# A delta-rule layer on one core: the chain over chunks in blocks of 4 steps with the decay added in PSUM, and the stage ahead of it spread over separate buffers

## The chip, the core and the metric

The kernel runs on one core of a Trainium2 chip. The metric is the device time of one execution, in microseconds (us), from launch to the last write. The core has a matmul engine (TensorE, PE in the profile; its weight loads are listed as PEld), a vector engine (DVE), a scalar engine (ACT), GpSimd (POOL) and a queue engine (SyncE, SP), which here issues nearly all of the DMA transfers. Each engine runs its own list of instructions and waits on semaphores.

## What is computed

Two transformer-like layers over 4096 tokens (two sequences of 2048) of width 256, all in float32 at the interfaces. The first is attention and a mixture of experts, the second a gated delta rule with 16 heads of width 16, a small MLP and a soft mixture of experts. The change touches the delta rule alone:

```python
def step(Sst, inp):
    q_t, k_t, v_t, b_t, g_t = inp
    Sst = Sst * g_t[..., None, None]                      # decay
    kS = jnp.einsum('bhk,bhkv->bhv', k_t, Sst)
    Sst = Sst + b_t[..., None, None] * jnp.einsum('bhk,bhv->bhkv', k_t, v_t - kS)
    o_t = jnp.einsum('bhk,bhkv->bhv', q_t, Sst)
    return (Sst, o_t)
_, out = jax.lax.scan(step, S0, (qt, kt, vt, bt, gt))     # over 2048 tokens of a sequence
```

## The kernel before

The program is a row of phases, each a function that hands every engine its own list of work; between phases all engines meet. The scan over tokens is done in chunks of 16 tokens (`CL`): within a chunk by products that need no earlier state, from chunk to chunk by a chain. Three phases prepare it (`phase_gram`, `phase_lanes`, `phase_mix`), and `phase_chain` runs the chain over the 128 chunks of a sequence, both sequences at once.

**phase_mix** goes over 32 tiles of 128 tokens. For a tile t, SP loads three tensors (`pr` L1942, `tp_in` L1943, `fac_in` L1945); ACT widens `tp_in` into `wide` (L2040); POOL scales k, v and q (L1973 to L1986); PE multiplies 64 blocks of 32x32 (`first`, L2004), ACT keeps the product in `nat` (L2047); PE multiplies 64 blocks again (`second`, L2016), DVE keeps that (L2070, L2072); PE turns two of the four results (L2024) and the decays (L2026) in the same stage as `second`, and ACT keeps them as `w_q` (L2054) and `gam_col` (L2056), the tables that the chain reads. SP stores `u_o` (L1951) and `k_end` (L1955). Inputs have two buffers, so the load of tile t waits until tile t-2 is scaled and widened; one set of PSUM tiles per parity (`ps`) is used by `first`, `second` and the turns in turn, so `first` of a tile waits until ACT has kept `w_q` of the tile before the last.

**phase_chain** keeps the state in SBUF in four sets (2 sequences x 2 halves of the heads). A step, for one chunk, is: PE multiplies the state by the chunk's `w` (L2182, 8 blocks of 32x32 for each sequence b), DVE subtracts that from `u_in` (L2226, one for each b), PE multiplies the result by `k_in` (L2192, 8 blocks for each b) into `ps_u`, and DVE makes the new state of b with two operations (L2233), one for each half of the 32 rows, as `ps_u` times a 0/1 mask plus `faded`. `faded` is the old state times the chunk's decay, made by ACT (L2209, four a step) beside it. Steps come in blocks of `CB` = 16; for each block SP issues 12 loads (L2131 two and L2133 one for each set) and 4 stores (L2142), and POOL copies the block's part of `w_q` and `gam_col` (L2162, L2163). All have two buffers: the load of block t waits until block t-2 is done.

`staged(eng, n, *stages, unroll=2)` (L87) writes an engine's list: stage s of round r works on tile r-s; `unroll` rounds stand in the body of a hardware loop (`Fori`, L101), and the rounds that don't fill the loop are written out before and behind it. So the body of PE's loop holds two tiles in phase_mix and two blocks, 32 steps, in phase_chain. A float32 32x32 product is two matmuls with a weight load each in the trace.

Rounds of SP in both phases: the load of round r, then the store of an earlier one, in that order.

Of the kernel before, what the change touches and what calls it, by code (L numbers as in the profile page):

```python
# [11 lines left out]
ALU = mybir.AluOpType  # L12
# [3 lines left out]
P = 128  # L16
D = 256
# [34 lines left out]
class Transfers:  # L52
# [24 lines left out]
    def before(self, t, p):  # L77

        return t * (16 * self.per) + (32 - 16 * p) * self.per
# [58 lines left out]
class Phase:  # L138
# [24 lines left out]
    def transfers(self, name, per=1, soft=False):  # L163
        return Transfers([self.sem(f"{name}{p}", soft) for p in range(2)], per, soft)
# [1724 lines left out]
def phase_mix(nc, sems, proj, t_p, factors, halves, w_q, gam_col, u_o, k_end, ident):  # L1889

    HG = H // 4
    with Phase(nc, "mix", sems) as ph:
        pr = ph.sb("pr", [P, 2, PW])
        tp_in = ph.sb("tp_in", [P, 2, 2 * H, CL])  # L1900
        fac_in = ph.sb("fac_in", [P, 2, 2, H])
# [5 lines left out]
        gam_k = ph.sb("gam_k", [P, 2, H, HD])  # L1907
# [4 lines left out]
        landed = ph.transfers("landed", 3)  # L1912
        widened = ph.steps("widened", 2)
        scaled = ph.steps("scaled", 6)
# [5 lines left out]
        w_q_kept = ph.steps("w_q_kept", KD + 1)  # L1920
# [12 lines left out]
        def _(sp):  # L1933
            for s in (landed, stored):
                s.prime(sp)

            def load(t, p):
                sp.wait_ge(scaled.sem, scaled.before(t))
                hold(sp, gate)
                sp.wait_ge(widened.sem, widened.before(t))  # L1940
# [7 lines left out]
            def store(t, p):  # L1948
                sp.wait_ge(y_kept.sem, y_kept.at(t))
                hold(sp, gate)  # L1950
                sp.dma_start(u_o[bass.ds(t * P, P)].rearrange("n a x -> n (a x)"),  # L1951
                             nat[:, p, 1:3].rearrange("q a h d -> q (a h d)")).then_inc(stored.sems[p], 32)
                sp.wait_ge(scaled.sem, scaled.at(t))
                hold(sp, gate)
                sp.dma_start(k_end[bass.ds(t * P, P), :], k_out[:, p].rearrange("q h d -> q (h d)")).then_inc(stored.sems[p], 32)  # L1955
            staged(sp, NT, load, idle, store)
# [4 lines left out]
        def _(pool):  # L1961
            scaled.prime(pool)

            def scale(t, p):
                q, k, v_in = [pr[:, p, i * D:(i + 1) * D].rearrange("q (h d) -> q h d", h=H) for i in range(3)]
                beta = pr[:, p, 3 * D:3 * D + H]

                def wide_of(x):
                    return x.unsqueeze(2).to_broadcast([P, H, HD])
# [3 lines left out]
                pool.tensor_tensor(b_gam[:, p, :], beta, fac_in[:, p, 0, :], ALU.mult).then_inc(scaled.sem, 1)  # L1973
                pool.tensor_tensor(k_v[:, p, :, 1, :], v_in, wide_of(beta), ALU.mult).then_inc(scaled.sem, 1)
                pool.wait_ge(scaled.sem, scaled.at(t, 1))
                hold(pool, gate)
                pool.tensor_tensor(k_v[:, p, :, 0, :], k, wide_of(b_gam[:, p, :]), ALU.mult).then_inc(scaled.sem, 1)  # L1977
                pool.wait_ge(y_kept.sem, y_kept.before(t))
                hold(pool, gate)
                pool.tensor_tensor(q_gam[:, p, :, :], q, wide_of(fac_in[:, p, 0, :]), ALU.mult).then_inc(scaled.sem, 1)  # L1980
                pool.wait_ge(turned.sem, turned.before(t))
                hold(pool, gate)
                pool.tensor_copy(gam_k[:, p, :, :], wide_of(fac_in[:, p, 0, :])).then_inc(scaled.sem, 1)
                pool.wait_ge(stored.sems[p], stored.before(t, p))
                hold(pool, gate)
                pool.tensor_tensor(k_out[:, p, :, :], k, wide_of(fac_in[:, p, 1, :]), ALU.mult).then_inc(scaled.sem, 1)  # L1986
            staged(pool, NT, scale)

        @block.tensor
        def _(pe):  # L1990
            for s in (firsts, seconds, turned):
                s.prime(pe)

            def first(t, p):
                pe.wait_ge(widened.sem, widened.at(t))
                pe.wait_ge(scaled.sem, scaled.at(t, 3))
# [1260 lines left out]
```

## Time and profile before

| | |
|---|---|
| median of 3 runs | 5107.75 us (5103.05 to 5109.47) |
| the profiled execution | 5108.61 us, of which its span is 5106.9 us |
| mean granted TensorE clock | 0.837 of full speed |
| busy over the span | PE 73%, PEld 39%, DVE 54%, ACT 41%, POOL 1172.7 us |
| instructions | 109157 |
| phase_mix, from PE's first product to the first memset of the chain | 3403.4 to 3638.2 us |
| phase_chain, from that memset to its last state | 3638.2 to about 4093.5 us |

Shares of busy time are means over a dozen phases, of which attention alone is 1.5 ms, so they say nothing on the two phases at hand; these are read by stretch. Idle time is given with what ended it; "issue" there means that an engine had nothing to wait for that the profile shows, and still did not go on. In lists in order of time, equal instructions are merged, and the second figure is how long the merged ones took from the first's start to the last's end.

### The profile page before, as it was taken

The page shows a single profiled execution, that of the slowest core. Times are in us where ns is not written, and L with a number is a line of the kernel's source. Part 1 is how long each engine was busy: PE and PEld are TensorE (multiplying, and loading weights), DVE is VectorE, ACT ScalarE, POOL GpSimd, SP SyncE. Part 2 cuts the span into 40 slices and gives each one's busy share as a digit, 9 for nine tenths or more (in the row PEclk, how much of TensorE's full clock was granted, in tenths as well). Part 3 has the DMA queues.
Part 4 walks back from the last instruction along what each step waited for, and adds up shares of the span by engine and source line. Part 5 has one row for each costly group of instructions (what it writes and reads, how often), then busy time and mean ns, then how long its engine had stood idle before and what let it go on. Part 6 is the DMA issues. An engine that isn't in the chain of part 4 may idle for free. (4 is left out here: it accounts for less than half of the span.)

```text
span 5106.9 us, 109157 instructions
## 1 busy us (share of the span) xinstructions
PE 3737.7 (73%) x37201; PEld 1984.0 (39%) x37203; DVE 2733.6 (54%) x5646; ACT 2108.3 (41%) x3466; POOL 1172.7 (23%) x2077
## 2 busy tenths in 40 slices
PE   6699999999999995528585447026444469789999
PEld 3233333333333332416363226016333346444478
DVE  5688888888888884812123654751133434423433
ACT  0177777777777774214242213013222212243322
POOL 4321121121122110162003730724200013311100
PEclk8799999999999997769797765557555579889999
DMA  1400000000000002044533323334433110040053
GB/s 44 168 35 0 0 0 0 0 0 0 0 0 0 0 0 78 25 156 152 173 119 103 116 84 122 90 106 161 86 42 46 23 56 4 11 157 25 4 186 131
DMA packets 256377, 319.78 MB, mean 63 GB/s; under 512 B 27729, under 2 KB 177489, under 8 KB 256209
## 3 DMA queue, kind: packets, MB, share of 16 engines
q1 hardware_dynamic: 243920, 283.86, 19.0%
q0 software_dynamic: 12288, 33.57, 2.0%
q8 instruction: 119, 1.95, 0.2%
q14 instruction: 50, 0.40, 0.0%
HBM read 181.58 MB, written 135.79 MB: 62 GB/s over the span
## 5 line engine op out<-in xcount | busy, mean ns | idle before, releaser
L791 DVE TENSOR_REDUCE att_maxes<-att_ps_m 128x1 f32<-128x512 f32 x2048 | 1342.0, 689 | 337.2 <-PE att_ps_m L648 324.0
L755 ACT ACTIVATE att_prob<-att_ps_s 128x1024 f32<-128x1024 f32 x1024 | 992.7, 1021 | 439.5 <-PE att_ps_s L658 429.5
L648 PE MATMUL att_ps_m<-att_k_t,att_q_t 96*128 96x512 bf16 x2048 | 792.8, 387 | 22.4 <-DVE att_maxes L791 4.8
L658 PE MATMUL att_ps_s<-att_q_t,att_k_t 99*128 99x512 bf16 x2048 | 612.6, 380 | 1.8 <-ACT att_q_t L741 1.7
L670 PE MATMUL att_ps_o<-att_prob,att_v_h 128*32 128x512 f32 x4096 | 546.3, 605 | 0.8 <-DVE att_o_sum L804 0.5
L648 PEld LDWEIGHTS att_ps_m<-att_k_t,att_q_t 96*128 96x128 bf16 x2048 | 196.6, 96 | 696.9 <-DVE att_maxes L791 595.0
L562 POOL CAST att_max_parts<-att_neg_max 128x4 bf16<-128x4 f32 x128 | 24.7, 193 | 1306.6 <-DVE att_neg_max L798 1306.6
L1359 DVE TENSOR_TENSOR experts_h<-experts_gs,experts_ps_g 128x128 f32<-128x128 f32 x192 | 55.4, 288 | 468.3 <-ACT experts_gs L1340 466.4
L658 PEld LDWEIGHTS att_ps_s<-att_q_t,att_k_t 99*128 99x128 bf16 x2048 | 190.7, 98 | 206.4 <-issue 31.7
L2209 ACT ACTIVATE chain_faded<-chain_state,chain_gam 128x32 f32<-128x32 f32 x512 | 126.6, 311 | 330.0 <-DVE chain_state L2233 320.6
L1312 PE MATMUL experts_ps_g<-w_gu,experts_x_t 128*128 x768 | 217.9, 406 | 35.6 <-ACT experts_x_t L1336 18.9
L2004 PE MATMUL mix_ps<-mix_k_v,mix_wide 32*32 32x32 f32 x4096 | 62.1, 236 | 241.7 <-POOL mix_k_v L1977 209.0
L2182 PE MATMUL chain_ps_w<-chain_state,chain_w 32*32 32x32 f32 x4096 | 96.6, 244 | 154.9 <-issue 85.6
L1575 PE MATMUL comb_ps_p<-comb_w_s,comb_h_t 128*128 128x512 f32 (+1 forms) x256 | 108.3, 583 | 129.4 <-DVE comb_pr L1530 123.0
L1305 PE MATMUL experts_ps_t<-ident,experts_xs 128*128 128x128 f32 x384 | 74.8, 278 | 165.6 <-DMA experts_xs<-slots_x 165.6
L2192 PE MATMUL chain_ps_u<-chain_u,chain_k_in 32*32 32x32 f32 x4096 | 95.0, 244 | 115.7 <-issue 89.6
L2233 DVE SCALAR_TENSOR_TENSOR chain_state<-chain_ps_u,halves,chain_faded 128x32 f32<-128x32 f32 x512 | 98.3, 245 | 130.2 <-PE chain_ps_u L2192 124.1
L1312 PEld LDWEIGHTS experts_ps_g<-w_gu,experts_x_t 128*128 128x128 f32 x768 | 131.3, 191 | 86.9 <-issue 76.1
L2226 DVE TENSOR_TENSOR chain_u<-chain_u_in,chain_ps_w 64x128 f32<-64x128 f32 x256 | 73.0, 285 | 160.2 <-PE chain_ps_w L2182 155.3
L2004 PEld LDWEIGHTS mix_ps<-mix_k_v,mix_wide 32*32 32x32 f32 x4096 | 58.6, 151 | 244.0 <-issue 244.0
L1466 POOL DMA_INDIRECT comb_y_in<-slots_y,pos x128 | 144.7, 1130 | 37.8 <-issue 36.6
L1336 ACT COPY experts_x_t<-experts_ps_t 128x256 f32<-128x256 f32 x192 | 72.4, 377 | 182.3 <-PE experts_ps_t L1305 181.8
(346 smaller groups left out, 6398.5 us busy)
## 6 DMA issues: line engine op xcount, KB each, us to landing
slots_x<-zeros SPq DMA_DIRECT2D x97, 256.0 KB, 3.3
experts_xs<-slots_x SPq DMA_DIRECT2D x48, 512.0 KB
slots_y<-experts_y SPq DMA_DIRECT2D x48, 512.0 KB
logits_t<-sstat_logit SPq DMA_DIRECT2D x64, 256.0 KB
xf_t<-logits_t SPq DMA_DIRECT2D x8, 2048.0 KB
proj<-comb_pr SPq DMA_DIRECT2D x8, 1600.0 KB
mix_pr<-proj SPq DMA_DIRECT2D x32, 400.0 KB
w_d<-in_L_ffn_wd SPq DMA_DIRECT2D x2, 4096.0 KB, 20.0
```

Source lines behind the costliest of these rows:

```text
L648: pe.matmul(ps_m[i % 2][:, :], q_t[0:PAIRS, p, tile * P:(tile + 1) * P], k_t[0:PAIRS, p, c * W:(c + 1) * W], start=True, stop=True).then_i ...
L658: mm = pe.matmul(ps_s[half][:, i * W:(i + 1) * W], k_t[0:ROWS, p, tile * P:(tile + 1) * P], q_t[0:ROWS, p, chunk * W:(chunk + 1) * W], sta ...
L670: mm = pe.matmul(ps_o[i * VW:(i + 1) * VW, :], v_h[:, p, group * GK + i, :], prob[:, (j * NH + i // 2) % RING, i % 2, :], start=(group == ...
L755: nc.scalar.activation(prob[:, i % RING, :, :].rearrange("q a w -> q (a w)"), ps_s[half][:, :], ACT.Exp, scale=SCALE).then_inc(expd.sem, 1)
L791: v.tensor_reduce(maxes[:, p, tile, c:c + 1], ps_m[i % 2][:, :], X, ALU.max).then_inc(reduced.sem, 1)
L1312: mm = pe.matmul(ps_g[p % 2][:, 0:2 * HID], x_t[:, p % 2, k, :], w_gu[:, k, bass.ds(e, 1), :, :].rearrange("q a i h -> q (a i h)"), start= ...
L1466: pool.indirect_dma_start(out=y_in[:, p, i, y, :], out_offset=None, in_=slots_y, in_offset=bass.IndirectOffsetOnAxis(ap=pos[:, t * GT + i, ...
L1575: mm = pe.matmul(ps_p[i % 2][:, a:b], h_t[:, k, i * P:(i + 1) * P], w_s[:, k, a:b], start=(k == 0), stop=(k == KD - 1))
L2004: mm = pe.matmul(ps[p][own, group, 32 * i:32 * i + 32], wide[own, p, place(h), :, :].rearrange("q a t -> q (a t)"), k_v[own, p, h, :, :].r ...
L2182: mm = pe.matmul(ps_w[32 * s:32 * s + 32, j, 0:32], w[own, p, s, c, :], state[own, c % 2, s, :, :].rearrange("q e d -> q (e d)"), start=Tr ...
L2209: nc.scalar.activation(faded[:, s, :, :], state[:, c % 2, s, :, :], ACT.Copy, scale=gam[:, p, s, c:c + 1]).then_inc(fades[b].sem, 1)
L2233: v.scalar_tensor_tensor(state[:, 1 - c % 2, sets, e, :], ps_u[:, sets, HD * e:HD * (e + 1)], halves[:, e:e + 1], faded[:, sets, e, :], AL ...
```

## The change

In phase_mix the three inputs get four buffers instead of two (`LOADS`), and the hardware loop holds four tiles instead of two on SP, POOL, PE and ACT. `first`, `second` and the turns write to PSUM tiles of their own (`ps_x`, `ps_y`, `ps_t`), and `turn` is a stage of its own, one tile behind `second`. The widening is split: four ACT operations of half the size, two ahead of `first` and two ahead of `second`. POOL's scaling is two stages. The decays are no longer turned tile by tile (`gam_k`, L1983, L2026 and L2056 go): one strided load fetches the decays of all chunks' ends at the phase's start, POOL widens them, PE turns them with four products, ACT keeps them at the end of the phase.

In phase_chain `CB` is 4 instead of 16, so SP's 16 transfers come every 4 steps, each a quarter of the size, and PE's loop body holds 8 steps. POOL makes, for each set, `fade`: a 32x32 diagonal matrix for each chunk and block of heads. In place of ACT's `faded`, PE multiplies the state by these diagonals (16 more blocks a step, between the two products of before) into `ps_u`, and the `k_in` product is added on top of it in PSUM. DVE's two operations for the new state of b become one, `ps_u` times a 0/1 mask. ACT has no work left in the phase.

```diff
-    HG = H // 4
+    LOADS = 4
...
+        ends = ph.sb("ends", [P, B, H])
+        ends_wide = ph.sb("ends_wide", [P, B, H, HD])
...
-        ps = [ph.ps(f"ps{i}", [P, HG, GP]) for i in range(2)]
+        ps_x = [ph.ps(f"ps_x{i}", [P, GP]) for i in range(2)]
+        ps_y = [ph.ps(f"ps_y{i}", [P, GP]) for i in range(2)]
+        ps_t = [ph.ps(f"ps_t{i}", [P, GP]) for i in range(2)]
+        ps_e = ph.ps("ps_e", [P, GP])
...
-            staged(sp, NT, load, idle, store)
+            staged(sp, NT, load, idle, idle, store, unroll=LOADS)
...
-            staged(pool, NT, scale)
+            staged(pool, NT, scale_kv, scale_qk, unroll=LOADS)
...
             def first(t, p):
-                pe.wait_ge(widened.sem, widened.at(t))
-                pe.wait_ge(scaled.sem, scaled.at(t, 3))
-                pe.wait_ge(w_q_kept.sem, w_q_kept.before(t))
+                pe.wait_ge(wide_t.sem, wide_t.at(t))
+                pe.wait_ge(kv_scaled.sem, kv_scaled.at(t))
+                pe.wait_ge(x_kept.sem, x_kept.before(t))
...
             def second(t, p):
                 pe.wait_ge(x_kept.sem, x_kept.at(t))
+                pe.wait_ge(wide_p.sem, wide_p.at(t))
+                pe.wait_ge(y_kept.sem, y_kept.before(t))
...
+            def turn(t, p):
                 pe.wait_ge(y_kept.sem, y_kept.at(t))
-                pe.wait_ge(scaled.sem, scaled.at(t, 5))
+                pe.wait_ge(w_q_kept.sem, w_q_kept.before(t))
...
-            staged(pe, NT, first, second)
+            staged(pe, NT, first, second, turn)
...
-            staged(act, NT, widen, keep_x, keep_w_q)
+            staged(act, NT, widen_t, idle, keep_x, idle, keep_w_q, unroll=LOADS)
...
-CB = 16
+CB = 4
...
-                    pool.tensor_copy(gam[:, p, s, :], gam_col[:, half, own]).then_inc(fetched.sem, 1)
+                    pool.tensor_tensor(fade[:, p, s, :, :], eye[:, :].unsqueeze(1).to_broadcast([P, CB, 32]),
+                                       gam_col[:, half, own].unsqueeze(2).to_broadcast([P, CB, 32]), ALU.mult).then_inc(fetched.sem, 1)
...
+                    for s in range(SETS):
+                        for j in range(4):
+                            own = slice(32 * j, 32 * j + 32)
+                            mm = pe.matmul(ps_u[own, s, 0:32], fade[own, p, s, c, :], state[own, c % 2, s, :, :].rearrange("q e d -> q (e d)"),
+                                           start=True, stop=False, skip_group_check=True)
+                    mm.then_inc(faded.sem, 1)
                     for b in range(B):
                         pe.wait_ge(us[b].sem, us[b].at(t, c + 1))
+                        pe.wait_ge(faded.sem, faded.at(t, c + 1))
...
                                 mm = pe.matmul(ps_u[32 * j:32 * j + 32, s, 0:32], k_in[own, p, c, cols], u[own, p, c, cols],
-                                               start=True, stop=True, skip_group_check=True)
+                                               start=False, stop=True, skip_group_check=True)
...
-            def chunks(t, p):
-                act.wait_ge(fetched.sem, fetched.at(t))
-                for c in range(CB):
-                    for b in range(B):
-                        act.wait_ge(states[b].sem, states[b].at(t, 2 * c))
-                        for s in range(KD * b, KD * b + KD):
-                            nc.scalar.activation(faded[:, s, :, :], state[:, c % 2, s, :, :], ACT.Copy,
-                                                 scale=gam[:, p, s, c:c + 1]).then_inc(fades[b].sem, 1)
...
-                        v.wait_ge(fades[b].sem, fades[b].at(t, KD * (c + 1)))
-                        for e in range(2):
-                            v.scalar_tensor_tensor(state[:, 1 - c % 2, sets, e, :], ps_u[:, sets, HD * e:HD * (e + 1)], halves[:, e:e + 1],
-                                                   faded[:, sets, e, :], ALU.mult, ALU.add).then_inc(states[b].sem, 1)
+                        v.tensor_tensor(state[:, 1 - c % 2, sets, :, :].rearrange("q s e d -> q s (e d)"), ps_u[:, sets, 0:32],
+                                        own_half[:, :, :].rearrange("q e d -> q (e d)").unsqueeze(1).to_broadcast([P, KD, 32]),
+                                        ALU.mult).then_inc(states[b].sem, 1)
```

## Rows read from the trace of the kernel before

**Rows 1.** Busy time by stretch: us, PE, PEld, DVE, ACT, POOL, clock, DMA share, GB/s

```profile
3403.00:3433.00 30.00, 17.21 (x912) 16.24 (x912) 2.27 (x6) 8.19 (x20) 12.08 (x25) 0.52 0.32 102
3433.00:3610.00 177.00, 116.71 (x6864) 112.35 (x6864) 19.00 (x51) 65.81 (x181) 75.47 (x153) 0.75 0.48 159
...
3657.00:3767.00 110.00, 46.92 (x2048) 34.15 (x2048) 42.58 (x192) 31.66 (x128) 4.64 (x13) 0.50 0.30 36
```

**Rows 2.** Order of time in the chain, one step: start, length, engine, line

```profile
3670.08 0.68 PE L2182 MATMUL chain_ps_w<-chain_state,chain_w 32*32 32x32 f32 x32 [0.52 <-DVE chain_state L2233]
3670.53 0.61 DVE L2226 TENSOR_TENSOR chain_u<-chain_u_in,chain_ps_w 64x128 f32<-64x128 f32 x2 [0.28 <-PE chain_ps_w L2182]
...
3670.96 0.69 PE L2192 MATMUL chain_ps_u<-chain_u,chain_k_in 32*32 32x32 f32 x32 [0.20 <-DVE chain_u L2226]
3671.50 0.73 DVE L2233 SCALAR_TENSOR_TENSOR chain_state<-chain_ps_u,halves,chain_faded 128x32 f32<-128x32 f32 x4 [0.36 <-PE chain_ps_u L2192]
...
3672.06 0.68 PE L2182 MATMUL chain_ps_w<-chain_state,chain_w 32*32 32x32 f32 x32 [0.41 <-DVE chain_state L2233]
```

**Rows 3.** Order of time in the chain, PE between two stops, and the longest stop

```profile
3675.47 0.53 PE L2192 MATMUL chain_ps_u<-chain_u,chain_k_in 32*32 32x32 f32 x28 [2.22 <-issue]
...
3678.52 0.67 PE L2182 MATMUL chain_ps_w<-chain_state,chain_w 32*32 32x32 f32 x31 [0.41 <-DVE chain_state L2233]
...
3681.09 0.21 PE L2182 MATMUL chain_ps_w<-chain_state,chain_w 32*32 32x32 f32 x1 [1.90 <-issue]
...
3785.95 0.53 PE L2192 MATMUL chain_ps_u<-chain_u,chain_k_in 32*32 32x32 f32 x28 [8.80 <-issue]
```

**Rows 4.** DMA queues from 3657 to 4094 us: packets, MB, share of 16 engines

```profile
q8 instruction: 71, 1.16, 1.2%
```

**Rows 5.** The same from 3403 to 3433 us, where phase_mix begins

```profile
q8 instruction: 5, 0.08, 1.2%
```

**Rows 6.** The same, all queues, from 3440 to 3610 us, the rest of phase_mix's loop

```profile
DMA packets 18000, 27.04 MB, mean 159 GB/s; under 512 B 5200, under 2 KB 8400, under 8 KB 18000
...
q1 hardware_dynamic: 18000, 27.04, 48.4%
```

**Rows 7.** The same, all queues, from 400 to 1850 us, in the attention

```profile
DMA packets 0, 0.00 MB, mean 0 GB/s; under 512 B 0, under 2 KB 0, under 8 KB 0
```

**Rows 8.** Groups of PE instructions from 400 to 1850 us: busy, mean ns, idle before

```profile
L648 PE MATMUL att_ps_m<-att_k_t,att_q_t 96*128 96x512 bf16 x1693 | 650.0, 384 | 14.9
...
L670 PE MATMUL att_ps_o<-att_prob,att_v_h 128*32 128x512 f32 x3392 | 451.7, 605 | 0.0
```

**Rows 9.** Order of time in phase_mix, one tile, all engines

```profile
3501.56 0.65 PE L2024 MATMUL mix_ps<-ident,mix_nat 128*128 128x128 f32 x4 [1.21 <-DVE mix_nat L2072]
...
3503.63 1.93 PE L2004 MATMUL mix_ps<-mix_k_v,mix_wide 32*32 32x32 f32 x128 [1.07 <-ACT gam_col L2056]
...
3504.39 0.36 SPq L1945 DMA_DIRECT2D mix_fac_in<-factors  x1
...
3505.33 1.79 PE L2016 MATMUL mix_ps<-mix_nat,mix_wide 32*32 32x32 f32 x128
3507.23 1.33 ACT L2040 ACTIVATE mix_wide<-mix_tp_in,halves 128x512 f32<-128x512 f32 x2 [3.74 <-DMA mix_fac_in<-factors]
```

**Rows 10.** Order of time at phase_mix's beginning, PE alone: one of its stops

```profile
3421.99 1.71 PE L2016 MATMUL mix_ps<-mix_nat,mix_wide 32*32 32x32 f32 x110 [2.70 <-issue]
```

**Rows 11.** Order of time, SP issuing the chain's transfers for one set after another

```profile
3718.27 0.86 SPq L2131 DMA_DIRECT2D chain_u_in<-u_o  x2
...
3719.84 0.86 SPq L2131 DMA_DIRECT2D chain_u_in<-u_o  x2
```

**Rows 12.** Order of time at the chain's start

```profile
3638.21 3.51 POOL L2151 MEMSET chain_k_in<- 128x4096 f32 x1 [17.08 <-POOLq L129]
...
3641.92 0.61 POOL L2162 COPY chain_w<-w_q 128x512 f32 x1
...
3657.80 0.53 PE L2182 MATMUL chain_ps_w<-chain_state,chain_w 32*32 32x32 f32 x32 [23.11 <-DMA chain_k_in<-k_end]
```

More of the change, by code:

```diff
@@ L77, in before @@
     def before(self, t, p):
-        return t * (16 * self.per) + (32 - 16 * p) * self.per
+        step = 32 // self.ring
+        return t * (step * self.per) + (32 - step * p) * self.per
 def hold(eng, gate):
@@ L161, in steps, with transfers @@
         return Steps(self.sem(name), per, ahead)
-    def transfers(self, name, per=1, soft=False):
-        return Transfers([self.sem(f"{name}{p}", soft) for p in range(2)], per, soft)
+    def transfers(self, name, per=1, soft=False, ring=2):
+        return Transfers([self.sem(f"{name}{p}", soft) for p in range(ring)], per, soft)
     def block(self):
@@ L1935, in _ @@
                 s.prime(sp)
+            with nc.allow_non_contiguous_dma("the decay at each chunk's end"):
+                sp.dma_start(ends[:, :, :], factors.rearrange("(i n t) a h -> n i t a h", i=B, t=CL)[:, :, CL - 1, 0, :]).then_inc(ends_in, 16)
             def load(t, p):
-                sp.wait_ge(scaled.sem, scaled.before(t))
+                sp.wait_ge(kv_scaled.sem, kv_scaled.before(t))
                 hold(sp, gate)
-                sp.wait_ge(widened.sem, widened.before(t))
+                sp.wait_ge(qk_scaled.sem, qk_scaled.before(t))
+                hold(sp, gate)
+                sp.wait_ge(wide_t.sem, wide_t.before(t))
+                hold(sp, gate)
+                sp.wait_ge(wide_p.sem, wide_p.before(t))
                 hold(sp, gate)
@@ L2028, in second, with widen @@
                 mm.then_inc(turned.sem, 1)
-            staged(pe, NT, first, second)
+            staged(pe, NT, first, second, turn)
         @block.scalar
         def _(act):
-            for s in (widened, x_kept, w_q_kept):
+            for s in (wide_t, wide_p, x_kept, w_q_kept):
                 s.prime(act)
-            def widen(t, p):
+            def widen(p, places, done):
+                for e in range(2):
+                    nc.scalar.activation(wide[:, p % 2, places, e, :], tp_in[:, p, places, :], ACT.Copy, scale=halves[:, e:e + 1]).then_inc(done.sem, 1)
@@ L2106, in phase_chain @@
         k_us = [ph.steps(f"k_us{b}", CB) for b in range(B)]
-        fades = [ph.steps(f"fades{b}", KD * CB) for b in range(B)]
-        states = [ph.steps(f"states{b}", 2 * CB) for b in range(B)]
+        faded = ph.steps("faded", CB)
+        states = [ph.steps(f"states{b}", CB) for b in range(B)]
         stored = ph.transfers("stored", SETS)
@@ L2118, in _ @@
                 s.prime(sp)
[L2119 removed]
+            sp.wait_ge(cleared, 7)
             def load(t, p):
@@ L2167, in _ @@
         def _(pe):
-            for s in w_s + k_us:
+            for s in w_s + k_us + [faded]:
                 s.prime(pe)
-            pe.wait_ge(cleared, 2)
+            pe.wait_ge(cleared, 7)
             def chunks(t, p):
@@ L2216, in _ @@
                 s.prime(v)
-            v.wait_ge(cleared, 2)
+            v.tensor_copy(own_half[:, :, :], halves[:, :].unsqueeze(2).to_broadcast([P, 2, HD])).then_inc(cleared, 1)
+            for j in range(4):
+                own = slice(32 * j, 32 * j + 32)
+                v.tensor_copy(eye[own, :], ident[own, own]).then_inc(cleared, 1)
+            v.wait_ge(cleared, 7)
             def chunks(t, p):
```

145 lines of the change are left out of this document (74 added, 71 removed).

## The prediction

> **What bounds the kernel now.** I read the page's order of phases first, then busy time by stretch, then lists in order of time inside the two phases, and last the DMA queues by stretch. In the chain PE is busy 46.92 of 110 us and DVE 42.58 [rows 1]: nobody is full, so it is either a chain of waits or something else. The list of a step shows the chain of waits [rows 2]: a step is PE's product with the state (3670.08), DVE's difference (3670.53), PE's product with `k_in` (3670.96), DVE's new state (3671.50), and the next step begins at 3672.06, 1.98 us later. 128 steps of 1.98 would be 253 us. From the first product (3657.80, [rows 12]) to the last state it is 436 us. The other 183 us are PE's stops [rows 3]: PE stops with "issue", no semaphore pending, for 2.22 us, runs 28 + 64 + 31 = 123 matmuls with as many weight loads, stops for 1.90 us, and so on; after every 122 or 123 pairs, wherever in a step that falls. The longest, 8.80 us, lies in a burst of 12 loads. The queue named "instruction" moved 71 packets of 16.4 KB (1.16 MB) in these 437 us [rows 4], one for each 6.2 us, which is the distance of the stops. So I read a stop as PE having no instructions: one packet holds some 122 pairs and the step's waits. The loop's body is 32 steps of 64 pairs, 2048 pairs, 16.8 packets, and goes round 4 times; 71 packets are 17.8 for each time round. It is fetched anew each time.
>
> That isn't so everywhere. In the attention no packet at all is moved in 1450 us [rows 7]. The pass of that loop handles two heads, 128 products of L648, of the 1693 in the window [rows 8]; with L658 (as many), L670 (3392) and the turns of keys, queries, maxima and outputs, some 641 pairs a pass, 5.3 packets and the waits more. Phase_mix's loop, 2 tiles of 264 pairs (128 of L2004, 128 of L2016, 8 turns), moves five instruction packets at its beginning [rows 5] and none in the rest of it: all 18000 packets there are the data queue's [rows 6]. So a body of 5.3 packets stays with PE, one of 16.8 doesn't. The limit is between.
>
> Phase_mix itself goes at 6.8 us a tile (6864 matmuls of 264 a tile in 177 us, [rows 1]), of which PE has 1.70 us from the start of `first` to that of `second`, as much for `second`, and 0.65 for the four turns [rows 9]. ACT waits 3.74 us for the load issued at 3504.39 and used at 3507.23: two buffers, a landing of 2.8 us and the work on a tile stand in a row. The phase is 235 us (3403.4 to 3638.2).
>
> **The chain, part by part.** (a) The `fade` products: 32 pairs a step, 0.53 us at 16 ns a pair (28 pairs in 0.53 us with their tail, [rows 2, 3]). They stand between the two products, where PE now waits for DVE from 0.55 to 0.88 us of the step; so 0.33 us is covered. PE also waits for their end before `k_in`'s product adds to them; behind that wait stand both `k_in` products, and DVE waits for these. From the step's start: products with the state until 0.55, fades until 1.07, the last one's end 0.2 later, so `k_in`'s product at 1.33 instead of 0.88. (b) ACT's `faded` goes: it ran beside PE and DVE and ended first (DVE waits for PE there, [rows 2]), worth 0. (c) The new state of b is one operation of 64 columns, not two of 32: the present four take 0.73 us, one of 128 columns (L2226) 0.3. b's first is 0.54 after its product begins, at 1.87, and lasts 0.25 to 0.3 with 0.1 to PE: the next step at about 2.28 us. 4 steps are 9.1 us. (d) Transfers: per block still 12 loads and 4 stores, now in 4 steps. SP gives out three loads in 1.57 us [rows 11], 12 in 6.3; 4 stores about 1.9. Load of block t+1 is free when block t-1 is done, stands behind the stores of t-1 (which begin some 0.9 us before the block's end), and its last one needs 2.4 us to land (2.8 from the start of issue [rows 9], less 0.36). From block end to landed: 1.2 + 6.3 + 2.4 = 9.9 us. That is more than 9.1, so SP sets the pace: about 10.0 us a block, 32 blocks, 320 us. Bounds: 9.2 (PE's chain alone) and 11.2 (no overlap of the stores), 294 and 358. (e) POOL's eight operations of 128 columns a block are under 0.62 each (a copy of 512 [rows 12]), under 5 us of 10, hidden; they'd cost 1 us a block only if they doubled. (f) Instructions: a body of 8 steps of 96 pairs is 768 pairs, 6.3 packets. I take it that it stays, since it is next to the attention's 5.3; only the first pass is fetched, 6 stops of 2.2, 13 us. (g) The start: 19.6 us from memset to first product [rows 12]; the memset is a quarter (0.9 instead of 3.5), and a first block of 12 small loads takes 6.3 + 2.4, in all 11 us. Sum: 11 + 13 + 320 = 344 instead of 455 us: **-111 us**, between -77 and -141.
>
> **Phase_mix, part by part.** (a) With four input buffers the landing of 2.8 us is out of the way, and with a PSUM set for each use nobody waits for `w_q`. ACT's work is 65.81 us for 26 tiles, 2.5 a tile (two operations more now, say 2.9), POOL's 75.47, 2.9 a tile, and SP's 5 transfers at 0.52 each [rows 11] 2.6, all under PE's: 1.70 + 1.70 + 0.5, and the turns 0.4 longer where the clock is at its lower level of 1.2 GHz, as it was in the first 30 us (0.52 [rows 1]). I take 4.3 us a tile, 138 us for 32. (b) The turning of the decays, 4 pairs and one ACT copy a tile, goes; in PE's 4.3 it is counted out. The new load of all decays stands first in SP's queue, and POOL's widening of it ahead of POOL's first tile, where behind it the loads of the tiles wait to land anyway: at most 1 us, once. Of the added waits, `second` waits for ACT's second widening, `x_kept` and DVE's `y_kept` of two tiles before: behind it on PE's queue stand the turn and the next `first`. ACT needs some 2 us from `first`'s end to `x_kept`; between them PE now has a turn and another tile's `first`, 2.2 us, and every stop makes that slack larger. I cost it at 0; without that cover it would be some 0.5 us a tile, 16 us. (c) Instructions. The body is now four tiles of 260 pairs: 1040 pairs, at 122 to 125 a packet 8.3 to 8.5, touching 9 or 10 packets. Ahead of the loop stand 3 batches of 64 products (one packet each), behind it 5. This is the step on which the sum hangs. Does a body of 8.4 packets stay? The rows that bound it are 5.3 (stays) and 16.8 (doesn't), and 8.4 lies nearer to 5.3 by the difference. I still take it as not staying, because a store of whole packets is most simply one of 8, and a body that touches 9 or 10 in turn then loses each before it comes back to it. Each packet costs a stop: 2.2, 1.9, 2.70 [rows 3, 10], and in data traffic say 2.5, and nothing else of PE's work is left to hide it. Packets: 3 + 7 passes of 10 + 5 = 78, 195 us. Sum: 138 + 195 + 5 for the first landing and the last copies = 338 instead of 235: **+103 us**. Bounds: stops of 1.9 give +56, of 3.5 give +181; none but the first pass, see the second rival.
>
> By the rows alone, 5.3 and 16.8 packets, both outcomes are open. The Trainium skill speaks against this change: Runtime: NRT & Kernel Launch, "Instruction fetch mechanics", says that PE's instruction memory is a first-in-first-out store of 128 KiB, 2048 instructions, in blocks of 16 KiB. The packets' size agrees; the capacity no row shows. Its next sentence, that crossing a block is mostly hidden, the trace contradicts with its 1.9 to 2.7 us. By that capacity the new body of phase_mix, 2080 instructions and its waits, doesn't stay, and that of the chain does.
>
> **The sum.** The profiled execution is 5108.6 us (span 5106.9), within 1 us of the median of 5107.75. 5108.6 - 111 + 103 = 5100.6. Later phases see the same inputs, the same clock level at their start and a few packets at other places: 0, give or take 3. Forecast **5101 us**, no change that can be told (0.2%, 10 us, is about what a measurement of this kernel tells from none). Its own range, with both terms' errors taken together, is 5050 to 5160.
>
> **Rivals.** First, slower: the fetch shares the DMA engines with data. There is a stop of 8.80 us inside a burst of loads [rows 3], and phase_mix moves 159 GB/s at a share of 0.48 [rows 1, 6], four loads ahead. If a fetch waits 1 us more on average (3.5 instead of 2.5), 78 of them add 78 us: 5179. It decides from 2.6 us a stop on. Against it: the stop of 2.70 was in such traffic [rows 10]. Second, the body stays: then phase_mix pays only 18 first packets, 138 + 45 + 5 = 188, -47, and the kernel is at 5108.6 - 111 - 47 = 4951. Third, in between: only those packets are lost that share a place with another, say 5 or 6 of 10 each pass, 11.5 us a pass after the first: 188 + 69 = 257, +22, and 5020. Fourth, the new chain's 6.3 packets don't stay either: its 100 packets at 6.2 us are 620 us, +175 over the present chain; 5390. Against it, the attention's body of at least 5.3.
>
> **How the numbers follow.** The forecast case 0.50, the slower fetch 0.12, the body stays 0.15, in between 0.19, the chain's body lost 0.04. Faster by over 0.2%: the body stays and in between (0.34) and a third of the forecast case (0.17), 0.51. Within 0.2%: 0.13, of the forecast case. Slower: the rest of the forecast case (0.20), the slower fetch and the lost chain, 0.36. The range for 8 in 10 leaves out the lost chain, the upper half of the slower fetch and the lower half of "the body stays": 4948 to 5182.
>
> **What would show it.** In the changed profile: in the chain no instruction packets after the first pass, steps of 2.3 us inside a block and a wait for a load of some 0.9 us at each fourth; PE's `k_in` product 1.3 us after the step's start. In phase_mix PE's stops with "issue" after each 122 to 125 pairs, some 70 instruction packets over the phase, a tile each 10 to 11 us. No packets there, and tiles of 4.3 to 5 us, would make the prediction wrong by 150 us downward; stops over 3.5 us, or packets in every pass of the chain, upward.

## The result, and the profile after

After takes **4908.29 us** (4905.81 to 4912.93), before 5107.08: 0.9613 of it, 95% interval 0.9596 to 0.9629, 199 us less. The forecast of 5101 and its range from 4948 are both missed.

Every stage time below is the distance between the starts of the first and the last instruction of PE in that stage's trace, its weight loads counted; it has nothing of the setting up between stages.

| stage | before | after |
|---|---|---|
| mix begins | 3397 | 3394 |
| mix | 237 | 196 |
| chain | 448 | 300 |
| mlp begins | 4114 | 3916 |

So the chain gave 148 us, phase_mix 41, the handovers around them 5, and mix begins 3 to 4 us earlier: 197 or 198. Behind mlp's beginning the two traces differ by less than 2 us. Where mix begins says nothing on the change: in the traces below (the second group's aside, where an earlier stage is longer) it is between 3388 and 3402 us, though the phases ahead of it are the same in all, and what moves it is open. So a few us between two kernels are evidence for a part of the change only where its own stage shows them.

One correction first: the text ahead of the prediction says that the hardware loop of phase_mix "holds four tiles instead of two on SP, POOL, PE and ACT", and the prediction has "the body is now four tiles". **For PE that is wrong.** The code of after has `staged(pe, NT, first, second, turn)`, without `unroll=LOADS`; PE's body is still two tiles, 520 pairs, 4.2 packets. SP, POOL and ACT have four. The word of three lists was carried over to the fourth.

The page's row of the instruction queue, of after (before had 119 there); then the same queue in 3403 to 3433 us, the beginning of phase_mix, which answers to [rows 5]; then all queues from 3433 to 3580, which answers to [rows 6]:

```profile
q8 instruction: 54, 0.88, 0.1%
```

```profile
q8 instruction: 6, 0.10, 1.4%
```

```profile
q1 hardware_dynamic: 18000, 27.04, 55.9%
```

That is 65 packets fewer, and in phase_mix none behind the first passes: in the third view the queue "instruction" has no line at all. Busy time by stretch, the columns of [rows 1], two stretches of phase_mix and one of the chain:

```profile
3403.00:3433.00 30.00, 18.97 (x1137) 16.87 (x1136) 3.02 (x8) 10.04 (x29) 11.10 (x22) 0.61 0.39 125
3433.00:3580.00 147.00, 97.72 (x6629) 87.95 (x6630) 18.88 (x50) 71.59 (x206) 65.03 (x127) 0.80 0.56 184
3660.00:3770.00 110.00, 74.98 (x4702) 64.80 (x4703) 47.56 (x196) 0.00 (x0) 29.06 (x96) 0.50 0.23 58
```

In the chain PE runs 4702 matmuls in the 110 us in which it ran 2048, a third of them the new products with the diagonals; counted in steps, it runs 49 (the 196 operations of DVE are 4 a step) instead of 32.

The chain of after in order of time, which answers to [rows 2]: SP's last load and its stores, a block's first product (3656.46), its second step (3658.40) and the beginning of its third (3660.33):

```profile
3654.57 0.34 SPq L2157 DMA_DIRECT2D chain_k_in<-k_end  x1
...
3655.32 1.94 SPq L2166 DMA_DIRECT2D delta_out<-chain_u  x4
3656.46 0.50 PE L2207 MATMUL chain_ps_w<-chain_state,chain_w 32*32 32x32 f32 x25 [1.72 <-POOL chain_fade L2187]
...
3657.69 0.90 SPq L2155 DMA_DIRECT2D chain_u_in<-u_o  x2
...
3658.40 0.48 PE L2207 MATMUL chain_ps_w<-chain_state,chain_w 32*32 32x32 f32 x25 [0.30 <-DVE chain_state L2251]
...
3658.71 0.69 PE L2213 MATMUL chain_ps_u<-chain_state,chain_fade 32*32 32x32 f32 x31
...
3659.50 0.53 PE L2224 MATMUL chain_ps_u<-chain_u,chain_k_in 32*32 32x32 f32 x32
3659.96 0.40 DVE L2251 TENSOR_TENSOR chain_state<-chain_ps_u,chain_own_half 128x64 f32<-128x64 f32 x2 [0.51 <-PE chain_ps_u L2224]
...
3660.33 0.48 PE L2207 MATMUL chain_ps_w<-chain_state,chain_w 32*32 32x32 f32 x25 [0.30 <-DVE chain_state L2251]
```

A step is 1.93 us (3658.40 to 3660.33); the product with `k_in` begins 1.10 into it. At each block's start PE waits some 1.7 us. The row names POOL's diagonals; but the last load was issued at 3654.57, and 1.89 us later PE begins. I read this wait as one for a load, and e7 below bears that out. SP has hardly any idle time in a block: 4 stores take 1.94 us, then 0.4 pass, 12 loads take 6.2, then 0.4 pass, in all 9.0.

Phase_mix of after, two tiles, which answers to [rows 9]:

```profile
3510.58 0.42 DVE L2094 TENSOR_TENSOR mix_nat<-mix_ps_y,mix_q_gam 128x256 f32<-128x256 f32 x1 [7.25 <-PE mix_ps_y L2035]
3510.92 0.41 DVE L2095 COPY mix_nat<-mix_ps_y 128x256 f32<-128x256 f32 x1
3511.10 1.93 PE L2023 MATMUL mix_ps_x<-mix_k_v,mix_wide 32*32 32x32 f32 x128
...
3511.57 0.38 SPq L1962 DMA_DIRECT2D u_o<-mix_nat  x1
...
3512.28 0.38 SPq L1966 DMA_DIRECT2D k_end<-mix_k_out  x1
...
3514.43 0.36 SPq L1956 DMA_DIRECT2D mix_fac_in<-factors  x1
...
3517.23 1.70 ACT L2056 ACTIVATE mix_wide<-mix_tp_in,halves 128x256 f32<-128x256 f32 x4 [4.76 <-DMA mix_fac_in<-factors]
...
3518.84 0.62 ACT L2070 COPY mix_nat<-mix_ps_x 128x256 f32<-128x256 f32 x2
...
3519.81 1.28 PE L2035 MATMUL mix_ps_y<-mix_nat,mix_wide 32*32 32x32 f32 x128 [3.08 <-ACT mix_nat L2070]
```

The next keep of DVE on the same parity is at 3521.53, 10.95 us after the first row. On average two tiles take 11.6 (6629 matmuls of 260 a tile in 147 us are 5.8 a tile). I read the rows as a **circle over two tiles**: DVE keeps tile t (3510.58), SP's stores wait for it, the loads of tile t+4 stand behind them in SP's queue and end at 3514.43, they land 2.8 us later, ACT widens (1.70), and only behind that in ACT's list stands the keep of the first products of tile t+2 (3518.84), for which PE's second product waits 3.08 us. Over the phase that wait is the largest that PE has:

```profile
PE mix_ps_y L2035 <- ACT mix_nat L2070: 52.5, 22, 4.1
```

Four buffers instead of two did not take the landing off the path: in both lists, SP's and ACT's, the path goes through an instruction that only happens to stand ahead.

### The profile page after: what moved, and what is told of

Read it like the earlier page. It is cut to its first block and busy times, and to the rows that moved or that the text cites. A ratio compares the mean times of both kernels' runs of the same rounds, so it can differ in the third digit from the quotient of the medians.

```text
span 4908.0 us, 117656 instructions
## 1 busy us (share of the span) xinstructions
PE 3725.7 (76%) x41174; PEld 1987.8 (41%) x41175; DVE 2681.0 (55%) x5395; ACT 1988.3 (41%) x2987; POOL 1202.6 (25%) x2238
## 5 line engine op out<-in xcount | busy, mean ns | idle before, releaser
L370 PE MATMUL qkv_ps_q<-qkv_w_t,qkv_xn_t 128*128 128x512 f32 (+1 forms) x256 | 104.8, 571 | 57.0 <-DVE v_sb L306 50.6
L1194 POOL DMA_INDIRECT slots_x<-z_sb,pos x128 | 123.1, 962 | 84.9 <-issue 84.9
L2207 PE MATMUL chain_ps_w<-chain_state,chain_w 32*32 32x32 f32 x4096 | 70.0, 244 | 90.3 <-DMA chain_k_in<-k_end 32.6
L671 PEld LDWEIGHTS att_ps_o<-att_prob,att_v_h 128*32 128x32 f32 x4096 | 80.8, 108 | 130.3 <-issue 81.8
L1326 PE MATMUL experts_ps_y<-w_d,experts_h_t 128*128 x384 | 125.9, 410 | 7.7 <-issue 3.7
```

What stands on the lines that cost most here:

```text
L370: mm = pe.matmul(ps_q[i % 2][:, a:b], xn_t[:, k, i * P:(i + 1) * P], w_t[:, k, a:b], start=(k == 0), stop=(k == KD - 1))
L671: mm = pe.matmul(ps_o[i * VW:(i + 1) * VW, :], v_h[:, p, group * GK + i, :], prob[:, (j * NH + i // 2) % RING, i % 2, :], start=(group == ...
L1194: pool.indirect_dma_start(out=slots_x, out_offset=bass.IndirectOffsetOnAxis(ap=pos[:, t, g, r:r + 1], axis=0), in_=xn_sb[:, t, :], in_offs ...
L1326: pe.matmul(ps_y[p % 2][:, 0:D], h_t[:, p % 2, :], w_d[:, bass.ds(e, 1), :].rearrange("q a c -> q (a c)"), start=True, stop=True).then_inc ...
```

## The experiments

Three groups of four runs, each beside runs of before. In the second group before takes 5184 us (on that chip the experts stage is 551 us long in the traces, elsewhere 476), so ratios to before are compared. The last two columns are stage times in us; in before they are 237 and 448.

| run | ratio to before | 95% | instruction packets | mix | chain |
|---|---|---|---|---|---|
| after | 0.9613 | 0.9596-0.9629 | 54 | 196 | 300 |
| e1_chain_alone | 0.9680 | 0.9664-0.9696 | 54 | 237 | 296 |
| e2_mix_alone | 0.9936 | 0.9919-0.9952 | 118 | 199 | 451 |
| e3_before_cb4 | 0.9678 | 0.9662-0.9694 | 52 | 239 | 296 |
| e5_pe_four_tiles | 0.9839 | 0.9822-0.9855 | 122 | 309 | 297 |
| e3b_before_cb8 | 0.9895 | 0.9878-0.9911 | 119 | 236 | 407 |
| e6_fades_half_twice | 0.9839 | 0.9823-0.9856 | 118 | 199 | 418 |
| e7_stores_on_act | 0.9559 | 0.9543-0.9575 | 54 | 194 | 266 |
| e10_old_chain_act | 0.9547 | 0.9531-0.9563 | 52 | 199 | 267 |
| e8_store_later | 0.9515 | 0.9499-0.9531 | 54 | 148 | 299 |
| e8b_keepx_near | 0.9517 | 0.9501-0.9533 | 54 | 151 | 299 |
| e9_both | 0.9466 | 0.9450-0.9481 | 54 | 153 | 267 |
| e11_old_chain_near | 0.9450 | 0.9435-0.9466 | 52 | 150 | 267 |

**Which part of the change.** e1_chain_alone is after with the old `phase_mix`, e2_mix_alone after with the old `phase_chain`.

> The new phase_chain with the old phase_mix. If the two stages are separate and the chain is what the trace of after says: chain 304 us instead of 455, total about 5107 - 151 = 4956 us (4945 to 4970). If part of that gain were mix's doing (w_q or the decay columns earlier), the total stays above 4975.

> The new phase_mix with the old phase_chain. By the trace of after, mix ends 37 to 45 us earlier: total 5062 to 5072 us, at a pace of about 11.6 us per two tiles, with instruction packets only in the first passes. By the prediction's term (a body of four tiles on PE, fetched anew in each pass) it would be slower than before, at about 5200 us; the code says PE kept a body of two tiles, so this should fall.

They take 4944.34 and 5076.61 us, where before takes 5108.53: -164 and -32, together -196 of after's -199. The two parts add up, and mix alone isn't slower, though its time is 5 us above the range expected; that of the chain alone is 1 us below its range. Of the 164, 152 lie in the chain and 6 in an earlier start of the experts stage, whose cause is open. No run separates the parts of the change in phase_mix (the PSUM tiles, the buffers, the decays): which of them brought its gain isn't shown.

**What in the chain.** e3_before_cb4 is one line:

```diff
-CB = 16
+CB = 4
```

> The kernel before with only CB changed from 16 to 4: same products, same two state operations a set, no diagonals, no merged update. Theory 1 (the chain's gain is instruction fetch: a body of a quarter of the length stays, and SP's 16 transfers a block, 9.1 us, set the pace from then on): the same chain time as with the new chain, 300 to 310 us, total 4950 to 4965 us. Theory 2 (the gain is the diagonals and the one masked update): total above 5070 us. In between, the difference from the run of the new chain alone is the price of the rest of the change.

This gives 4942.71 us against 4944.34 with the whole new chain: the same, and 7 us below the range expected; the chain's 296 us are a little below the 300 to 310 as well. Theory 2 falls. The diagonals, the products with them and the masked update bring nothing that these runs can tell; **the whole gain is the length of the block**. That length sets two things at once, the body of PE's loop and the size of the loads; the next group of runs takes them apart. The trace of e3_before_cb4, first all queues from 3660 to 3900 us, then its steps:

```profile
q1 hardware_dynamic: 33760, 13.86, 22.2%
q8 instruction: 1, 0.02, 0.0%
```

```profile
3700.08 0.53 PE L2182 MATMUL chain_ps_w<-chain_state,chain_w 32*32 32x32 f32 x32 [1.45 <-POOL chain_gam L2163]
...
3702.07 0.68 PE L2182 MATMUL chain_ps_w<-chain_state,chain_w 32*32 32x32 f32 x32 [0.42 <-DVE chain_state L2233]
...
3704.05 0.68 PE L2182 MATMUL chain_ps_w<-chain_state,chain_w 32*32 32x32 f32 x32 [0.40 <-DVE chain_state L2233]
...
3706.02 0.68 PE L2182 MATMUL chain_ps_w<-chain_state,chain_w 32*32 32x32 f32 x32 [0.40 <-DVE chain_state L2233]
...
3708.94 0.54 PE L2182 MATMUL chain_ps_w<-chain_state,chain_w 32*32 32x32 f32 x32 [1.35 <-POOL chain_w L2162]
```

There is one packet in 240 us instead of one for every 6.2 us, the step is 1.98 us as it was in [rows 2], and a block takes 8.9 us: SP's pace hides any difference of the step. Before had 67 packets more and took 166 us more, 2.5 us each.

**How long a body may be.** e5_pe_four_tiles builds what the prediction took the change to be:

```diff
-            staged(pe, NT, first, second, turn)
+            staged(pe, NT, first, second, turn, unroll=LOADS)
```

(with `p % 2` where PE reads `nat`). e3b_before_cb8 is before with `CB = 8`. e6_fades_half_twice makes half of the products with the diagonals twice in each step, 24 products instead of 16 (its expectation says "pairs"; in the prediction's count a product is two pairs, so 896 pairs a body instead of 768):

```diff
-                    for s in range(SETS):
+                    for s in (0, 1, 0, 1, 2, 3):
```

> After, with PE's loop in phase_mix unrolled over four tiles instead of two: the body that the prediction wrongly took the change to have, 1040 product and load pairs, about 8.4 packets. Theory 1 (as the prediction priced it: it doesn't stay): about 60 to 70 packets more in mix, 2.5 us each, total 5040 to 5070 us. Rival (8.4 packets stay, like the 5 to 6 of attention and of the new chain): within 5 us of after (4905 to 4915), with packets in the first pass only.

> The kernel before with CB = 8 instead of 16: half the body (PE's runs through the chain would be about 8.4 packets long), twice as many passes, so the same number of packets in all if the body is fetched anew each time. Theory 1 (a body must be shorter than that to stay; the run with four tiles on PE showed 68 packets more at a like length): within 15 us of before, 5095 to 5120 us, about 119 packets. Theory 2 (the gain of the short blocks comes from something else that falls with CB, such as the loads' landing or POOL's copies at a block's start): about halfway, 5020 to 5040 us.

> After, with half of the products with the diagonals made twice in each step (the same values again): 24 instead of 16 pairs, PE's body of the chain longer by a sixth, 7.2 instead of 6.2 packets, which touch 8 packets of 16 KB. Theory 1 (8 packets stay, more don't): within 5 us of after, 4905 to 4915 us, 54 to 56 packets, the products being hidden under the wait for the transfers. Rival (the bound is below 8): 60 to 110 packets more and 100 us or more slower.

**e5** takes 5027.21 us, 68 packets and 119 us more than after, with phase_mix at 309 us. Theory 1 has the packets right: a body of 8.4 doesn't stay. The time is 13 us below its range, which had counted 2.5 us a packet. PE's waits in phase_mix of e5 (us in total, times, longest), then two queues in 3433 to 3690 us:

```profile
PE mix_ps_x L2023 <- issue: 64.8, 38, 3.3
PE mix_ps_y L2035 <- issue: 57.6, 32, 2.1
```

```profile
q1 hardware_dynamic: 19008, 28.52, 35.9%
q8 instruction: 66, 1.08, 2.0%
```

These are 70 stops, 122 us, 1.75 each. In their shadow the waits for ACT's keep shrink from 52 us to 7; on the other side PE is busy 172 us instead of 128 in the phase, at a granted clock of 0.50 instead of 0.76. With the 10 us of stops that after has itself, that makes the 113 us by which phase_mix is longer.

**e6**: theory 1, that 8 packets stay, falls. The ratio is 0.0226 above after's, 115 us at 5108, with 64 packets more. From 3730 to 4100 us, behind the first pass, the queue moved 63 in 15 passes, 4.2 a pass:

```profile
q8 instruction: 63, 1.03, 1.4%
```

They don't come evenly. PE's waits in one pass (3792.6 to 3822.5 us), then in the next (3823 to 3844.5):

```profile
PE chain_ps_w L2207 <- issue: 8.7, 4, 5.3
PE chain_ps_u L2213 <- issue: 5.8, 3, 2.4
PE chain_ps_u L2224 <- issue: 2.0, 1, 2.0
```

```profile
PE chain_ps_w L2207 <- DVE chain_state L2251: 2.5, 8, 0.5
```

So it goes on: a pass with 8 stops, then one with none, 9 packets for the two; the whole chain has 63 stops, 126 us in all. In the trace, 6.3 packets stay; of 7.3 every second pass is fetched anew; of 8.4 every pass. Why the passes alternate is open. The Trainium skill (Runtime: NRT & Kernel Launch, "Instruction fetch mechanics") gives PE a first-in-first-out store of 2048 instructions; the body of 896 pairs, 1792 matmuls and loads, is below that, and was still fetched anew every second time. The measurement decides: that a body is shorter than the store was not enough here.

**e3b**: the packets are as theory 1 says, 119 like before, but it takes 54 us less (at 5108), outside of the 15 that theory 1 allows and short of the 68 to 88 of theory 2. The rest is in the length of the stops. PE's waits in the chain, of before, then of e3b:

```profile
PE chain_ps_u L2192 <- issue: 89.6, 28, 8.8
PE chain_ps_w L2182 <- issue: 85.6, 39, 4.7
...
PE chain_ps_w L2182 <- DMA chain_k_in<-k_end: 23.1, 1, 23.1
```

```profile
PE chain_ps_w L2182 <- issue: 120.4, 55, 4.4
...
PE chain_ps_u L2192 <- issue: 18.7, 9, 2.8
PE chain_ps_w L2182 <- DMA chain_k_in<-k_end: 14.3, 1, 14.3
```

Before has 175 us of stops and e3b 139, none over 4.4, and 9 us less to the first load: 45 us, where the chain is 41 shorter. Before's longest stop, 8.8, lies in a burst of 12 large loads [rows 3]; with loads half the size such stops are gone. That the loads hold the packets up is what these rows suggest; no run moved the loads alone. So of the 166 us of e3, some 36 may be owed to smaller loads and not to fewer packets; e5 and e6, in which the body grows and the loads stay as they are, show by themselves that the packets cost.

**What bounds the chain now, and what the diagonals are worth there.** e7_stores_on_act is after with `store` of phase_chain moved from SP's list to ACT's. e10_old_chain_act is the same with the old step in blocks of 4, where ACT's stores of block t-1 stand between its decays of steps 2 and 3:

```diff
+                    if c == 2 and not fresh:
+                        store(t - 1, 1 - p)
```

> After, with the chain's four stores a block issued by ACT, which has nothing to do there, instead of SP. Theory 1 (SP's 16 issues of 0.5 us set the block's pace of 9.1 us): SP is left with 12 loads of 0.52 us, 6.2 us, and they land 1.9 us after the last, 8.1 us; PE's four steps take 7.7. Pace 8.1 to 8.3 us a block, 26 to 32 us off, total 4876 to 4883 us. Theory 2 (what the rows name, POOL's copies and diagonals at a block's start, sets it): no change, 4905 to 4912 us.

> The new phase_mix with the old way of a step (decayed state made by ACT, two state operations a set) in blocks of 4, the stores issued by ACT between its decay operations. It asks whether the diagonals are worth something once SP is off the path. ACT has 16 operations of 0.31 us and 4 stores of 0.5 us in a block, 6.9 us. Theory 1 (the step hangs on PE and DVE in both forms, 1.98 against 1.93 us): 0 to 8 us slower than after with its stores on ACT. Theory 2 (ACT's stores hold its decay back, once a block, by up to 1.2 us): 30 to 40 us slower than that.

e7 has 0.9559 against after's 0.9613, 28 us at 5108, and its chain is 266 us instead of 300. That is theory 1, and the name POOL in the rows of after was the wrong one. SP's and PE's rows of e7: SP's first and last loads of a block and the first of the next, then PE's first product of two blocks in a row:

```profile
3778.22 0.87 SPq L2154 DMA_DIRECT2D chain_u_in<-u_o  x2
...
3783.96 0.34 SPq L2156 DMA_DIRECT2D chain_k_in<-k_end  x1
3785.97 0.96 SPq L2154 DMA_DIRECT2D chain_u_in<-u_o  x2
```

```profile
3778.21 0.48 PE L2213 MATMUL chain_ps_w<-chain_state,chain_w 32*32 32x32 f32 x25 [0.29 <-DVE chain_state L2257]
...
3786.12 0.48 PE L2213 MATMUL chain_ps_w<-chain_state,chain_w 32*32 32x32 f32 x25 [0.47 <-DVE chain_state L2257]
```

A block takes 7.75 to 7.9 us, which is PE's own four steps and up to 0.2 us, and SP is idle in between. And here, where a step would count, e10 with the old one has 0.9547 and a chain of 267 us: **the diagonals are worth nothing even there.** They cost nothing either: e10 is 6 us faster where 0 to 8 slower was expected, which is within the intervals of 0.0016 (8 us) on each side. Theory 2 of e10 falls too.

**The circle in phase_mix.** Two runs cut it at different places:

```diff
-            staged(sp, NT, load, idle, idle, store, unroll=LOADS)
+            staged(sp, NT, load, idle, idle, idle, store, unroll=LOADS)
```

```diff
-            staged(act, NT, widen_t, idle, keep_x, idle, keep_w_q, unroll=LOADS)
+            staged(act, NT, widen_t, keep_x, idle, keep_w_q, unroll=LOADS)
```

> After, with SP's stores of phase_mix moved one tile later (a tile's stores are issued behind the loads of the tile five on instead of four on). Theory 1 (a circle over two tiles sets the pace of 5.8 us a tile: DVE's keep of tile t, SP's stores of t, the loads of t+4 queued behind them, 2.8 us landing, ACT's widening of t+4, behind it ACT's keep of tile t+2, PE's second product, DVE's keep): the circle is then three tiles long and the pace falls to what PE and the transfers allow, 4.3 to 4.8 us, 32 to 45 us off, total 4863 to 4876 us (on a chip like the first; 0.952 to 0.955 of before). Theory 2 (the loads wait for the transfers themselves): no change, 0.960 to 0.963.

> After, with ACT's keeping of the first products one tile behind its widening instead of two (the list widen_t, keep_x, idle, keep_w_q), SP's as it was. It cuts the same circle at another place: the keep of tile t+2 no longer stands behind the widening of t+4 but of t+3. Theory 1: as with the stores moved, 32 to 45 us off, 0.952 to 0.955 of before. Theory 2 (the circle is not the cause, or ACT now waits for PE's first product instead): 0.960 to 0.963, or up to 20 us slower.

The ratios are 0.9515 and 0.9517 (4862.23 and 4864.15 us), with phase_mix at 148 and 151 us instead of 196. Both come out as theory 1 has it, with ratios a little beyond its range. PE's wait for ACT is still there in e8_store_later, but small. The first row is that wait over the phase, the next two are two tiles in order of time, 4.00 us apart, the last is its stretch from 3433 to 3530 us:

```profile
PE mix_ps_y L2035 <- ACT mix_nat L2070: 19.9, 25, 1.7
```

```profile
3490.62 1.28 PE L2035 MATMUL mix_ps_y<-mix_nat,mix_wide 32*32 32x32 f32 x128 [0.68 <-ACT mix_nat L2070]
...
3494.62 1.28 PE L2035 MATMUL mix_ps_y<-mix_nat,mix_wide 32*32 32x32 f32 x128 [0.92 <-ACT mix_nat L2070]
```

```profile
3433.00:3530.00 97.00, 76.91 (x6404) 69.32 (x6399) 18.36 (x49) 68.22 (x198) 62.87 (x125) 1.00 0.84 271
```

**Both together.** e9_both is e7 with e8b's list, e11_old_chain_near is e10 with it.

> After, with both moves: the chain's stores on ACT and ACT's keeping one tile behind in mix. If the two don't touch each other: 27 us off from the chain and 32 to 45 us from mix, 0.947 to 0.950 of before, a mean of 4845 us where before takes 5108. If the chain starts later because mix's last stores now collide with it, less than the sum.

> The same two moves with the old way of a step in the chain (ACT decays, two state operations) in blocks of 4. The run with the old step and ACT's stores had 0.9547 against 0.9559 with the diagonals, intervals of 0.0016 each side: if the diagonals are worth nothing in either form, this and the run before it agree within 8 us, 0.946 to 0.950.

They take 4837.00 and 4828.75 us. By the ratios that is 75 and 83 us below after (0.0147 and 0.0163 at 5108), where the gains one by one, 28 and 49, make 77: they add. Both ratios are just below the ranges expected, e11's by 0.001. The kernel with the old step is 8 us faster (4826.16 to 4832.12 against 4835.51 to 4838.73), but not in the chain, 267 us in both; in its trace mix begins 5 us earlier and is 3 shorter, in code that is the same in the two, and why is open. The version that beats both kernels has none of the diagonals.

## Why the prediction was wrong

**The step that failed is (c) of phase_mix.** "The body is now four tiles of 260 pairs" is a misreading of the diff, and +195 us of packets hung on it. What the runs showed in its place: PE's body stayed at two tiles, 4.2 packets, no packet was fetched behind the first passes, and the changed phase_mix took 41 us less, not 103 more. This was no risk of the machine: the rival "the body stays" was weighed at 0.15 as if the chip were in doubt, when the code had the answer. The cost that the step puts on such a body is borne out: e5 is that kernel, and with the same new chain it is 83 us over e1, which has the old phase_mix (5027 against 4944), where the step says +103, between +56 and +181. It fetched 10 packets in a pass, as the step has it, and 76 in the phase instead of 78. That the sum came so near is in part luck: a stop was 1.75 us, not 2.5, so they took 122 us and not 195, but between the stops a tile took 5.8 us, not 4.3, at a granted clock of 0.50.

The other steps, in the prediction's order:

**Bound of the chain.** 183 us are stops for instruction packets, one packet for each: right in the main. The waits put down to "issue" are 175 us in 67 stops (the rows of before at e3b), against 71 packets; e3, e5 and e6 show that they come and go with the packets, and e3b that their length isn't the packets' alone.

**(a), (c) of the chain, the step.** I predicted 2.28 us and 1.93 were measured. The `k_in` product begins at 1.10, not 1.33: I added 0.2 us for the last product's end to a time by row lengths, which already held it. From there to the next step it took 0.83 us instead of 0.95. The old step is 1.98, so the new one isn't slower, as the sum had it, but 0.05 faster, and either way it is hidden under SP.

**(b)** ACT's decay operations worth 0: right (e3, e10).

**(d), the pace.** SP sets it: right. Its size is 9.0 instead of 10.0, which is 32 us over 32 blocks. I laid the block's end, stores, loads and 2.4 us of landing in one chain. But SP begins its stores 0.4 us after its last load, before that has landed; the landing (1.9) delays PE, not SP. Once the stores are gone from SP's list (e7), the last load, issued at 3783.96, would land at 3785.86 by that 1.9, and PE begins its block at 3786.12: the landing is hidden there too.

**(e)** POOL hidden: right; POOL is busy 29 of 110 us. **(f)** The body of 6.3 packets stays, with 6 stops in the first pass: right, but they took 9.5 us in all, not 13. **(g)** It was 9 us from memset to first product instead of 11.

The chain, all in all, gave -148 by PE's instructions where -111 was predicted, beyond the bound of -141. (That bound is itself a slip: the terms 11 + 13 + 294 give -137, and 11 + 13 + 358 give -73.) From its memset to its last state it took 305 us instead of 344, and 32 of these 39 are (d).

**(a) of phase_mix.** I predicted 4.3 us a tile and 5.8 were measured. I priced the landing at nothing because four buffers stood there, and didn't follow which instruction stands ahead of which in SP's and ACT's lists. With the circle cut (e8) the tile takes 4.0 us, so PE's share was priced well. The missing wait was worth 48 us of the stage's time.

**(b)** The decays' turning and the added waits were costed at 0, covered by "2.2 us" of other work. In e8, where the circle is cut, PE still waits 0.7 to 0.9 us a tile for ACT (19.9 us over the phase), so that cover isn't whole.

**Rivals.** The second, the body stays, gave 4951 us by a mix of -47 (measured -41) and the chain's -111. It is nearest, though for a reason that it didn't name, and 43 us too high, with the chain 37 too high. So (c) put right would not have given the time: the size of (d) would still have been missing. The first (the fetch in data traffic waits 3.5 us) has nothing for it: a stop took 1.75 us in e5, with the data queue at 35.9%. The third, that about half of the packets is lost, has its like at 7.3 packets (e6), not at 8.4, and there as a whole pass lost and a whole pass kept, not as some packets in each. (Its price was a slip as well: 5 or 6 packets at 2.5 us are 12.5 to 15 us a pass, not 11.5.)

**The range** was widened for the chip's uncertainty alone. A sentence that a line of the code could have settled needs no chance; it needs the line. Where such a step carries the sign of the sum, quote the call of each engine's list beside the number.

## What to carry to other kernels

Count the instructions in the body of PE's hardware loop. Here a body of 6.3 packets of 16 KB ran without a fetch behind its first pass, one of 7.3 was fetched anew in every second pass and one of 8.4 in every pass, at 1.75 to 2.5 us a packet; a change of one constant was worth 3.2% of the kernel. Before an operation is restructured, try the length alone: the diagonals and the masked update, most of the chain's diff, did nothing that shows. And more buffers shorten no wait that comes through the order of an in-order list: follow the list from the wait back to whatever stands ahead of the load.

## What the runs showed of the hardware that I had not expected

Between a loop body that stays and one that doesn't there is a state in between: at 7.3 packets a pass with 8 stops and a pass with none took turns, 9 packets for the two. The price of a packet depends on its surroundings: 2.5 us in the old chain, 2.0 in e6, 1.75 in e5, and up to 8.8 in a burst of large loads [rows 3].

The granted clock of TensorE in phase_mix rose with the pace: 0.75 before [rows 1], 0.80 in after, 1.00 in e8_store_later from 3433 to 3530 us, where PE is busy 0.79 of the time instead of 0.66. The 128 matmuls of a tile's product take 1.93 us in some tiles of after and 1.28 in others (its rows at 3511.10 and 3519.81), and 1.28 in e8 at 1.00, the higher of the two levels (2.4 GHz); so cutting a wait there went along with shorter work. In e5, where PE was busy 143 of 257 us (0.56), it was 0.50. In the chain the clock was 0.50 throughout, in after as in before, though PE's share of busy time rose from 0.43 to 0.68.
